# A two-layer decoder on one core: a new order of the two lanes on every engine, and wait blocks merged into their first steps

## What is computed

```python
x = ln(x + attn_rel(x))                  # A: blocks of 128 tokens, clipped relative positions
x = ln(x + xattn(x, ctx))                # X0: 77 context rows, boolean mask
x = ln(x + ffn_one_expert(x))            # F0: one of 8 experts, chosen per sequence
x = ln(x + bump_attention(x))            # BU: weights max(0, 1 - |k - q| / bandwidth)
x = ln(x + xattn(x, ctx))                # X1: second cross attention, integer mask
for l in range(2):                       # inside L1_ffn
    x = x + causal_attn(ln(x))           # S0, S1: masked scores, softmax, 16 heads
    x = x + moe(ln(x))                   # M0: all 8 experts per token; M1: 2 chosen per sequence
x = ln(x)
```

## Time and profile before

| | |
|---|---|
| median of 3 runs | 1359.96 us (1358.13 to 1365.36) |
| the profiled execution, first to last instruction | 1360.6 us |
| mean granted PE clock in it | 0.871 of 2.4 GHz |
| PE busy / weight loads | 1153.6 us (85%) / 651.8 us (48%) |
| DVE, ACT, POOL busy | 761.6 us (56%), 657.0 us (48%), 339.0 us (25%) |
| DMA engines | 57.85 MB, mean busy share 0.16 |

### The profile page before, as it was taken

One profiled execution on the slowest core, in us unless ns is written; L12 is line 12 of the kernel. 1 busy time (PEld: TensorE's weight loads), 2 busy tenths in 40 slices (PEclk: granted clock), 3 DMA queues, 4 the chain that ended last, 5 costly groups with the idle time before them and its releaser, 6 DMA issues.

```text
span 1360.6 us, 19642 instructions
## 1 busy us (share of the span) xinstructions
PE 1153.6 (85%) x7254; PEld 651.8 (48%) x7254; DVE 761.6 (56%) x1977; ACT 657.0 (48%) x1132; POOL 339.0 (25%) x735
## 2 busy tenths in 40 slices
PE   7949577789789999979997867778879999988986
PEld 6934321353344567744465431333334467764455
DVE  4654685557595421278345577577587332159443
ACT  2116279615238643316743549844317743323861
POOL 3032210233335200034503121042424300032520
PEclk9759578759699999989998967788779989989998
DMA  7040000120430000070024100021330000033011
GB/s 248 1 109 14 10 1 1 38 73 7 106 91 3 4 1 1 1 186 3 3 63 114 34 1 1 3 69 39 98 98 4 3 2 1 0 113 75 3 42 37
DMA packets 48348, 57.85 MB, mean 43 GB/s; under 512 B 16469, under 2 KB 41349, under 8 KB 47750
## 3 DMA queue, kind: packets, MB, share of 16 engines
q1 hardware_dynamic: 47390, 56.13, 15.3%
q10 hardware_dynamic: 864, 0.48, 0.1%
HBM read 35.13 MB, written 20.87 MB: 41 GB/s over the span
## 4 chain that ended last, share of the span: by engine, by line
PE 63%; DVE 20%; ACT 10%; POOL 3%; issue 3%; DMA 2%; SPq 0%; ACTq 0%; POOLq 0%; DVEq 0%
PE banks L1616 10%; PE banks L1606 10%; ACT sb_arena L1299 6%; PE banks L1422 5%; PE banks L1410 5%; DVE sb_rmax L1551 5%; PE banks L1397 3%; PE banks L957 2%; PE banks L470 2%; PE banks L1249 2%; PE banks L605 2%; PE banks L1275 2%; PE banks L465 2%; POOL sb_rstd L461 1%; PE banks L675 1%
## 5 line engine op out<-in xcount | busy, mean ns | idle before, releaser
L1551 DVE TENSOR_REDUCE sb_rmax<-banks 128x1 f32<-128x384 f32 (+3 forms) x352 | 204.8, 637 | 73.8 <-PE banks L1399 73.4
L1480 ACT ACTIVATE sb_arena<-banks 128x512 f32<-128x512 f32 x320 | 175.2, 597 | 94.6 <-PE banks L1410 93.7
L1299 ACT ACTIVATE sb_arena<-banks,sb_zk 128x512 f32<-128x512 f32 x256 | 152.7, 821 | 22.2 <-PE banks L1249 20.9
L1397 PE MATMUL banks<-sb_arena,sb_qs 128*128 128x128 bf16 (+3 forms) x512 | 131.0, 325 | 25.2 <-DVE sb_rmax L1551 19.6
L1671 ACT ACTIVATE sb_arena<-banks,sb_b 128x512 f32<-128x512 f32 x128 | 87.3, 687 | 132.9 <-PE banks L1606 131.6
L460 POOL TENSOR_SCALAR sb_var<-sb_mv 128x4 f32<-128x4 f32 x40 | 10.3, 258 | 562.0 <-DVE sb_mv L445 561.9
L1616 PEld LDWEIGHTS banks<-sb_w,sb_arena 128*128 128x128 f32 x1024 | 126.4, 193 | 32.7 <-issue 32.7
L1509 POOL TENSOR_SCALAR_AFFINE_SELECT sb_arena<-sb_arena 128x256 f32<-128x256 f32 x256 | 99.1, 408 | 172.2 <-ACT sb_arena L1480 172.2
L1730 DVE SCALAR_TENSOR_TENSOR sb_xall<-banks,sb_region,sb_xall 128x128 f32<-128x128 f32 x160 | 44.9, 344 | 157.8 <-PE banks L1616 157.8
L1616 PE MATMUL banks<-sb_w,sb_arena 128*128 128x128 f32 x1024 | 127.1, 276 | 0.0
L1606 PE MATMUL banks<-sb_ft,sb_w 128*128 128x512 f32 x256 | 126.6, 607 | 0.0
(11 more groups left out here) (281 smaller groups left out, 1888.0 us busy)
## 6 DMA issues: line engine op xcount, KB each, us to landing
sb_qs<-q_scratch SPq DMA_DIRECT2D x32, 288.0 KB, 4.8
q_scratch<-sb_region SPq DMA_DIRECT2D x16, 384.0 KB, 2.5
sb_arena<-k_scratch SPq DMA_DIRECT2D x16, 288.0 KB, 6.9
sb_arena<-in_chosen SPq DMA_DIRECT2D x8, 514.0 KB, 4.3
sb_w<-in_w SPq DMA_DIRECT2D x2, 2048.0 KB
q_scratch<-sb_region SPq DMA_DIRECT2D x16, 256.0 KB, 2.1
sb_qs<-q_scratch SPq DMA_DIRECT2D x32, 96.0 KB, 2.3
k_scratch<-sb_region SPq DMA_DIRECT2D x8, 384.0 KB, 2.6
```

The costliest lines, as they stand in the source:

```text
L1299: i = nc.scalar.activation(L.dist[h % 3][:, kb, :], (b2_, b3)[h % 2], ACT.Abs, bias=L.zk[:, kb, h:h + 1])
L1397: nc.tensor.matmul(o[:, i * kl:(i + 1) * kl], L.qs[:, h // 2, t * 128:kl], L.ks[:, key_of(h), 0:kl], start=(i == 0), stop=False)
L1480: nc.scalar.activation(L.probs[:, u % SLOTS, :], bank_of(SELF_ORDER, ring, ("key", u)), ACT.Exp)\
L1551: nc.vector.tensor_reduce(L.rmax[:, t, g * GROUP + h0:g * GROUP + h0 + nh], bank_of(SELF_ORDER, ring, ("max", step))[:, 0:nh * kl] .rearra ...
```

## The change

It does three things.

1. All five strings in `ORDER` are new: SP, PE, ACT, POOL and DVE. The number of steps is the same on each engine apart from what follows.
2. In `cross_tensor` and in `self_tensor` the `yield` between the wait block and the first bank goes (`if step: yield`). The waits then stand in the step that fills the first bank; PE has eight steps fewer for each lane.
3. In `cross_pool` the `yield` ahead of the wait on `k32` goes in X1, and the one behind the split moves inside the condition. In X0 the settled wait and the mask work are one step; in X1 the settled wait and the first part of the split are one. That is one step fewer for each cross stage.

No instruction is added or removed. Decoded, the new strings give this: the same stages of the two lanes still run side by side, steps are moved by less than one place on the mean and by about twelve at most. On PE 501 of 1872 working steps come ahead of a step that they used to follow; on DVE 242 of 1025, on ACT 165 of 909, on POOL 53 of 350. The order of the first steps of PE in S0, as an example, with the lane before the stage and the number of the step behind it: after 0S0.5, 0S0.6 and 0S0.7 (lane 0's banks) come 1S0.28 and 1S0.29, which is lane 1's first key unit, and then 0S0.8; before, lane 0's banks up to 0S0.14 came ahead of that unit. In S1 and in both stages of the second round the unit passes three of lane 0's banks. At the end of BU, lane 1's step 1X1.3 (a bank of cross scores) now stands ahead of 0BU.34 (L1249); in the second round 1X1.3 stands ahead of 0BU.32.

```diff
@@ -169,28 +169,28 @@
 ORDER = {
     "SP":
-    "2fa516bc1ff006fe01ac5fc06a67fe422f01ff801fe01ac5fc06a648",
+    "57a316cb8ff005fe01a9df405a67fe4418dd77007ee015cfb406a64a0",
     "PE":
-    "9455c0fcd8fffffe3c207039e07fc7ff9ff0fffce4400000000042eb6fdaf6cc333e4d502402dfffebffe0920496cbdad657"
...
+    "2a53c0fcd8ff1fe9bf4e84ac24dedfbfadbaf7def440000000008baebeedf15670cf398089383ffebfff43014938deace579"
...
     "ACT":
-    "c33336ffe001fe0f7dfbf8f9000002eb7aeaaaa906ffc7000fc76cdbfdfc8000407fffe00001fffc07dad932aeba6badfcf8"
...
+    "297336ded7e09c8dddbedb7b000008eb7b734cca0666cdf707c4acd777f96000356f6734cdc5aa8d266ad329ad767377e5c4"
...
     "POOL":
-    "81fc72729f98547ffff800007fff800ffe333338cf33cfffc006000007fffe00007fff800ff8f333398f3cf3ffc00400001f"
...
+    "4af1a5ca7d858ef7c036e77d56cce22bc8e66d97877aaa6c6b400100eebf5ed32b93b0f9c316cc78a56dfc91d663400001f2"
...
     "DVE":
-    "257096a955f47ffd9483fffffc00000007fad4a69ab8d4aa952f57ded57e505c66d8d99fffe0612190000ba07caffffa012a"
...
+    "2b10afc06df473ffb429687b717f3b005e02d4a69a74d91b194f67df55bd501d4ba69d9db2bb792184140520ef97dff16029"
...
@@ -967,7 +967,8 @@
             pe.wait_ge(*p.last("k_first"))
             pe.wait_ge(*p.last("q_first"))
             for step in range(CROSS_STEPS):
-                yield
+                if step:
+                    yield
                 if step == T:
                     pe.wait_ge(*p.last("q_rest"))
                 if step < G * T:
```

More of the change, by code:

```diff
@@ L171 @@
     "SP":
-    "2fa516bc1ff006fe01ac5fc06a67fe422f01ff801fe01ac5fc06a648",
+    "57a316cb8ff005fe01a9df405a67fe4418dd77007ee015cfb406a64a0",
     "PE":
-    "9455c0fcd8fffffe3c207039e07fc7ff9ff0fffce4400000000042eb6fdaf6cc333e4d502402dfffebffe0920496cbdad657"
-    "6bbaffffffe4d08000000040000a8ed5ffff800d6b773d576b73a8eb4d15b2db5acd87dadb67dc1cfe84d040000208880556"
-    "faaaaaaaaaaaaaab555552aab55404a81d5ffffe00a9addaeab6da7cc8faaa56d6d96b361fedb35b7703fa13410000080400"
-    "03dbfaaa0360ffbf7bf7ffffe3ffc3fe07ffe1c8100000202000000113aeefdd7db3e435409001ff36dff5fff424c24cb55c"
@@ L178 @@
-    "bdbf97fdffff96900000225000000000ff6b7ff80155776baadb69f323eaa95b5b65acd87fb6cd6ddc0fe84d040000208880"
-    "556faaaaaaaa555555555555555555502541d5ffffe00aab5daeab6da7cc8faaa56d6d96b361fedb376e703fa13410000080"
-    "40003dbfaaa8000",
+    "2a53c0fcd8ff1fe9bf4e84ac24dedfbfadbaf7def440000000008baebeedf15670cf398089383ffebfff43014938deace579"
+    "e97dfdffefb61040000000000870fda7ffe334253db6d6bd2eea3ad34c55e4d2ed5bd5ae77572a79b1b110000044294805bd"
+    "59530374e4e76197c15bb316f804320ec7fff58e09d9dcd59ebcda68f73296763b9d69b3bf43f3bc0c8d3f21000010100005"
@@ L181 @@
+    "fb7ce402e0fb7bfeffffff1f7cafcceabfe7c810000100080000024ebbbf5ed9d157e504405783efbfebffa1c4138ce6cbd7"
+    "6f37fff7ff6880002440200000000ffd9fdf03512eacfb2ed57a68f5b39a751bc6b4dffb184f6ca46ff112000004091a00af"
+    "b21d6c739b829da2a8da6c2d1aec04d079dffe95d06dd6b39e9f4f8a37d44bbcb53b56cc7e8dcff49342b6cc060000404000"
+    "3eefc63331204214",
     "ACT":
-    "c33336ffe001fe0f7dfbf8f9000002eb7aeaaaa906ffc7000fc76cdbfdfc8000407fffe00001fffc07dad932aeba6badfcf8"
-    "400200c1ee90d5aaaaaaaa817fffe00001fff80fd6aaaab6bab5d5fcf840020005ed807ffcf800fffffffc100080800b6df5"
@@ L184 @@
-    "eaa9037fe078007fc755ff7f4012ffff800000001fff80fd6aaaab6bab5d5fcf8400200c1ee90d555555555415ffff00001f"
-    "ff80fd6aaaab6bab5d9fcf840020005edc00",
+    "297336ded7e09c8dddbedb7b000008eb7b734cca0666cdf707c4acd777f96000356f6734cdc5aa8d266ad329ad767377e5c4"
+    "7001184c8ca92793a1b4cd82dcdf3f2e4736b4155a6aa5cf9b36ee7c95c0020011fa80dbf7bb7e3aefbbd4700080048375f5"
+    "e95886776a7959895c53ff7dc029ec346360063387c7be21666e2bb9b3c5fd8d1d00100ca599332e4e92d94a0d5d79ce3c3b"
+    "79df806749d4f5b1bb707e15c020009ed9400",
@@ L186 @@
     "POOL":
-    "81fc72729f98547ffff800007fff800ffe333338cf33cfffc006000007fffe00007fff800ff8f333398f3cf3ffc00400001f"
-    "8c63707f21c1ffffe00001fffe003fe3cccce63cf3cfff001800001ffff80001fffe003fe3cccce63cf3cfff0010000060",
+    "4af1a5ca7d858ef7c036e77d56cce22bc8e66d97877aaa6c6b400100eebf5ed32b93b0f9c316cc78a56dfc91d663400001f2"
+    "98bc1fa453fdd7eded906852d3c864f19766b875665dcb5040003dab786b99abb88df0dd6d8cb1bcb796e3329000005b028",
     "DVE":
-    "257096a955f47ffd9483fffffc00000007fad4a69ab8d4aa952f57ded57e505c66d8d99fffe0612190000ba07caffffa012a"
@@ L191 @@
-    "9555552b4a0007f21c8aaf7c1caffffe804aa52aaaa5aa8001fe807f361ffdf57fffff802828c000007e686955b96a92a5d2"
-    "febdb93fe30c33366ffff061219206000605df95fff002aa52aaaa5aa8001fc8722abde872bffffa024a94aaaa96aa0007fa"
-    "01fe00",
+    "2b10afc06df473ffb429687b717f3b005e02d4a69a74d91b194f67df55bd501d4ba69d9db2bb792184140520ef97dff16029"
+    "52d68b2b520007f05a29df3a1f2f7fcf0552a52a9655b24001ff00bf361fdfde7f4ffc457c140580c128706955aadb2345e1"
+    "ffb75c77c84caa7a7b5efdc288d0400e001abbf2fbe0245266a6a66b41001fc1709cbe7179bfef5709344cab1656aa0007f8"
@@ L194 @@
+    "0bd8b00",
 }
```

## The result

| | before | after |
|---|---|---|
| median | 1359.8 us (1358.1 to 1365.4, 4 runs) | 1393.6 us (1386.0 to 1398.4, 4 runs) |
| ratio after to before | | 1.0239, 95% interval 1.0201 to 1.0277 |
| profiled execution, span | 1360.6 us | 1384.2 us |
| mean granted PE clock of it | 0.871 | 0.874 |

The changed kernel is slower by 34 us. Forecast was +8, with a range up to 1382: right in sign, a quarter of the size.

What follows compares the result with a forecast made beforehand. PE was taken as full in M0 and ACT in the bump stage, leaving idle time at self attention entries. Gains -3.3, gates +8.2 and X1 +3.7 summed to +8.6, rounded down to +8: 1368 us, range 1344 to 1382.

Steps and rivals of the forecast that it cites:

- What bounds the kernel: Bump stage bound by ACT, M0 by PE; idle time that matters lies at self attention entries, not caught up behind.
- a sign of being wrong: M0 or the bump stage changing by more than 2 us would mean the prediction had missed the place.
- The moved waits: Wait blocks on PE and waits on POOL standing a step or two elsewhere: booked at 0 us.
- The entries at 0: Self attention entries: idle time filled by lane 1's work, lane 0's turn no earlier; booked 0, 13 us kept for lower end.
- The mechanism of the gate: Self attentions: lane 1's first key unit waits for its late stacking DMA, holding lane 0's banks behind it; sum +8.2 us.
- The size of the gate: Four self attentions: +2.9, +1.3, +2.4 and +1.6 us, sum +8.2, ends 0 and 11.8.
- the ring: At the gates: up to three banks filled ahead for DVE, 0.56 us each, a cover of 1.7 us.
- The entry of X1: Lane 1's fourth cross score bank waits for loads ahead of lane 0's bump steps: +3.2 us, second round +0.5.
- SP at 0: SP's list changes by single places, no load behind a later-met wait: 0, within 0.5 us either way.
- The clock: Stalls slow PE behind the gates; nothing in the sum as PE keeps ahead of DVE; 1 us per gate would give 1372.
- Gains: Rival: gates cost nothing and the 13.0 us at the self attention entries come through, 1348 us; chance 0.22.
- gates and clock: Rival: self attention gates without cover, X1 at its upper end, 4 us for the clock: +18.6, 1379 us; chance 0.10.

Runs made afterwards that it cites:

- the swap alone: Kernel before with only lane 1's first key unit moved on PE, ahead of 7, 3, 3 and 3 of lane 0's banks: 1363.5 us, ratio 1.0019.
- the old entries: Changed order everywhere except the entries of the four self attentions, which have the old order; waits kept as own steps: 1389.8 us, ratio 1.0214.
- the split: Changed kernel with lane 0's remaining q and k loads in each self attention issued behind the stacking of lane 1's first maxima: ratio 1.0128.
- both repairs: Changed order with lane 0's remaining self attention loads behind the stacking, and second X0's third stacking between the load groups: 1372.5 us, ratio 1.0075.

## Why the prediction was wrong, step by step

- **What bounds the kernel: right.** The first M0 and the bump stages kept their length within 1.4 us, the entries of the self attentions carried most of the loss, and what was lost there was not caught up in the full stretch behind. The second M0 got 3.9 us shorter, beyond the 2 us that I had named as a sign of being wrong; most of that is clock, as said above.
- **The moved waits: right**, shown by the run that has only them.
- **The entries at 0: right in the place.** PE's idle time before lane 0's turn fell from 2.69 to 0.41 us in S0 and from 5.12 to 0.67 in S1, but the turn came no earlier: 11.6 us behind the start of S0 (before 10.4) and 6.0 behind that of S1 (before 6.0).
- **The mechanism of the gate: right and shown.** The same DMA, the same place, the same queue, in all four stages, and issuing it earlier takes the stall away.
- **The size of the gate: the step that failed.** The four terms (2.9, 1.3, 2.4, 1.6) are lane 0's missing banks and 0.7 us for later loads, less a cover of up to 1.7 us from the ring. With the swap alone that is roughly what came: +3.4, +2.0, +1.0 and -1.0 us, 5.4 where 8.2 were booked. In the changed kernel the four stages lost 16.1 us, and 23 us in the times of the run with the new order in their windows alone. The terms held only for an order that is otherwise the old one: they left out that the other moved steps (501 on PE alone) also change how much work DVE still has when the gate closes. S0 shows it, changed kernel and then the run with the swap alone:

```profile
383.38 0.80 SPq L577 DMA_DIRECT2D sb_qs<-sb_mrows  x1
...
380.96 5.84 DVE L1552 TENSOR_REDUCE sb_rmax<-banks 128x1 f32<-128x384 f32 x10 [1.02 <-PE banks L1399]
```

```profile
382.00 0.79 SPq L577 DMA_DIRECT2D sb_qs<-sb_mrows  x1
...
385.98 1.28 DVE L1551 TENSOR_REDUCE sb_rmax<-banks 128x2 f32<-128x512 f32 x2
```

  In both DVE goes on some 8 us behind the issue (8.4 and 8.1). But it runs dry 3.4 us behind it in the changed kernel, at 386.80, and 5.3 us behind it, at 387.26, with the swap alone: hence 5.03 us of idle time instead of 2.83. With the old entries it runs dry 4.1 us behind the issue and is idle for 3.96. So the entries took a part of the cover and the other moved steps the rest. Being late counts for little: the DMA was issued 27.2 us behind the start of S0 instead of 25.8, but in the run with the self attentions alone, where it was issued after 25.0, DVE was still idle for 4.83. Cover does not explain all of the size. DVE's idle time at the gates grew by 6.2 us from the swap alone to the changed kernel, the four stages by 10.7. That the DMA carries most of it is shown by the split (16.1 to 2.5 us); how the rest of it comes about is open.
- **The entry of X1: right in place, wrong in effect.** Lane 1's bank waits there indeed, the longest wait but one of this kind:

```profile
270.56 0.41 PE L921 MATMUL banks<-sb_cbias,sb_identb 128*128 128x308 bf16 x1 [9.05 <-DMA sb_qs<-q_scratch]
...
271.16 1.94 PE L1249 MATMUL banks<-sb_arena 128*32 128x512 f32 x8
...
267.92 1.70 SPq L513 DMA_DIRECT2D sb_qs<-q_scratch  x4
```

  But the loads were issued at 267.92, 2.3 us earlier than before, and lane 0's bump stage ended at 278.0 instead of 278.3. I had taken the issue time as fixed. Steps moved on the other engines must have brought it forward; which ones was not tested. The 3.2 us did not come.
- **SP at 0: wrong.** The one swap in the second X0 (L577 behind the loads of q) made that stage 5 of its 6.3 us longer in the trace, as undoing it showed; the times can't show it. I had checked SP's list for loads behind late waits, and not for small DMAs behind large loads.
- **The clock: the term that I left out of the sum.** I had reckoned that DVE would hide it. S0 has 2.7 us more PE busy time for the same matmuls at 0.88 instead of 0.94, though 9 of their records are missing. But this slow work lies before 400 us, where PE is not the bound (0.74 instead of 0.96 from 380 to 400 us), and behind it the clock is 1.00 in both traces. So it is not shown that it cost S0 anything. Where PE is full, it did: 1.5 us more busy time and 1.4 us more stage in the first M0, at 0.97 instead of 0.99; with the split, in the same order, it was back at 118.5 us and 0.99. And the three executions that were not profiled, at 0.862 to 0.863, took 5 to 12 us longer than the profiled one at 0.874; that is most of the distance from the 23.6 us between the traces to the 34 between the medians. The Trainium skill, TensorE: Matmul & The Clock Gate, section What's actually happening, says that recent activity releases the throttle; by it a stall costs twice. The trace agrees in the direction in S0, and does not agree in the second X1, where the clock fell with PE busy (last section).
- **The rivals.** Gains came only outside the self attentions (first 356 us -1.3; second M0 -3.9, of which 1.4 us are idle time, 0.3 instead of 1.7). The pair gates and clock (1379) was the nearest. Its place was right, but it had nothing for the second X0, and its gates without any cover came to 11.8 us where 16.1 were lost.

What stays open: a third of the loss is left with both repairs. In that trace part lies in M1 (40.5 us, before 39.2) and the second X0 (65.3, before 61.8), part in the second S1, which stayed at 105.4 us against 102.3. I did not find the single step there. Another part is clock: the first X1 took 85.1 us at 0.66, with the same order on PE, DVE, ACT and POOL as in the changed kernel, where it took 78.1 at 0.80. Whether the new order itself lowers the clock, or the executions differ by chance, these few traces can't say. A run with one engine's whole new order alone was not tried: the lists hang together through their waits.

## What to carry to other kernels

A fixed order that looks ragged may be fitted to latencies: the old list reached each first key unit at most 1.7 us before its DMA landed. Before a waiting instruction is moved forward, take the time when its DMA lands with everything that is in the queue ahead of it, and not the DMA's usual landing time, and ask what work is left for the busy engine by then if all other steps have moved too. If such a gate hurts, changing the order in which the DMAs are issued (here one `yield`) took away nearly half of the loss.

## What I had not expected of the hardware

**The clock moves whole stages, with the order unchanged.** The second X1, in the old order each time, in the kernel before (74.1 us, clock 0.79), then with the new order in M1 and X0 alone, and then with the split and the moved key units:

```profile
908.11:988.50 80.39, 70.06 (x320) 30.12 (x318) 51.82 (x123) 28.70 (x51) 29.80 (x50) 0.70 0.16 48
```

```profile
906.35:987.79 81.44, 71.32 (x320) 30.15 (x318) 52.02 (x123) 28.59 (x51) 29.54 (x50) 0.69 0.16 46
```

PE works 7 to 8 us longer on 320 matmuls, its idle time is the same 10 to 11 us. In the run with only the self attentions new one sees the fall from 1.00 to 0.50 (from 2.4 to 1.2 GHz) in the middle of this stage, with PE busy for 3.80 and 3.90 of 4 us ahead of it:

```profile
941.00:945.00 4.00, 3.80 (x26) 1.23 (x25) 3.45 (x8) 2.17 (x5) 0.84 (x4) 1.00 0.00 0
945.00:949.00 4.00, 3.90 (x18) 1.07 (x18) 3.43 (x6) 3.33 (x7) 0.00 (x0) 0.84 0.01 2
949.00:953.00 4.00, 4.00 (x20) 0.87 (x13) 0.00 (x0) 1.10 (x2) 0.00 (x0) 0.50 0.00 0
```

That is 40 us behind the start of the stage; in the kernel before it came 54 us behind it (at 958). Over 33 executions of the kernel before the time ran from 1352.0 us at a mean clock of 0.883 to 1368.9 us at 0.871, correlation -0.94. The time thus goes with the clock; what sets the clock of an execution no run here shows. So a single trace can be off by 8 us in one stage, and a stage table should be read with its clock column.

**A small DMA waits for the large ones ahead.** The stacking DMA (L577) took 7.0 to 7.8 us to be felt behind eight loads, at most 4.0 us when four of them were issued after it. The first figures are those of PE's first matmul behind the gate: 7.0 in the second S0 of the kernel before, where PE waited for it, and 7.8 in S0 of the changed kernel; the last is S0 with the split, where PE did not wait.
